# A rolling pipeline of attention tiles: the turned maxima move into the bank of the projections, and rounds of the loop end elsewhere

## What is computed

```python
xn = rmsnorm(x, norm_w)
q = (xn @ wq).reshape(T, 4, 4, 32)          # 16 query heads in 4 groups
k, v = cond @ wk, cond @ wv                 # 4 heads of 32 shared by the groups
attn = softmax(q @ k.T / sqrt(32))          # 512 x 512 for each of 16 heads
out = x + (attn @ v).reshape(T, 512) @ wo
```

## Time and profile before

| | us |
|---|---|
| median of 3 runs | 4432.54 (4431.65 to 4432.71) |
| profiled execution, its own time | 4432.37 |
| its span, first to last instruction | 4430.5 |
| TensorE busy | 4158.9 (94%) |
| VectorE busy | 2515.7 (57%) |
| ScalarE busy | 2077.2 (47%) |
| GpSimd busy | 2008.8 (45%) |
| DMA, share of 16 engines | 36% |

### The profile page before, as it was taken

One profiled execution on the slowest core, in us unless ns is written; L12 is line 12 of the kernel. 1 busy time (PEld: TensorE's weight loads), 2 busy tenths in 40 slices (PEclk: granted clock), 3 DMA queues, 4 the chain that ended last, 5 costly groups with the idle time before them and its releaser, 6 DMA issues.

```text
span 4430.5 us, 62098 instructions
## 1 busy us (share of the span) xinstructions
PE 4158.9 (94%) x19496; PEld 2654.1 (60%) x19496; DVE 2515.7 (57%) x3453; ACT 2077.2 (47%) x2648; POOL 2008.8 (45%) x1072
## 2 busy tenths in 40 slices
PE   9999999988999999999788999998999999899999
PEld 7888888874665566555444554554555555454555
DVE  3122200016556655566577777777777777777775
ACT  2111211114344444444265666665666666656665
POOL 0000000004555555565256665655666566656665
PEclk9999999998999999999899999999999999999999
DMA  5333522235444554454322322323222333223322
GB/s 182 132 128 136 160 87 82 93 96 138 119 127 124 130 132 118 126 136 130 96 81 69 81 78 81 90 81 88 75 81 77 89 90 91 73 75 81 85 74 66
DMA packets 316045, 451.72 MB, mean 102 GB/s; under 512 B 45176, under 2 KB 117368, under 8 KB 315832
## 3 DMA queue, kind: packets, MB, share of 16 engines
q1 hardware_dynamic: 315832, 448.86, 36.0%
HBM read 217.72 MB, written 102.77 MB: 72 GB/s over the span
## 4 chain that ended last, share of the span: by engine, by line
PE 37%; DVE 5%; ACT 5%; issue 4%; SPq 0%; POOL 0%; DVEq 0%; DMA 0%; ACTq 0%
PE a_ps L2017 9%; PE a_ps L2063 7%; PE a_ps L2049 6%; PE a_ps L2006 6%; PE a_ps L2086 5%; DVE a_max_cols L1885 3%; ACT a_q_ops L1769 2%; PE a_ps L2074 2%; PE a_ps L2079 2%; ACT a_probs L1778 2%; PE a_ps L2040 1%; PE a_ps L1992 1%; DVE a_stage L1904 1%; DVE x_lo L1895 1%; DVE wq_lo L1862 0%
## 5 line engine op out<-in xcount | busy, mean ns | idle before, releaser
L1885 DVE TENSOR_REDUCE a_max_cols<-a_ps 128x1 f32<-128x512 f32 x1536 | 1022.5, 672 | 421.2 <-PE a_ps L2017 415.4
L1778 ACT ACTIVATE a_probs<-a_ps 128x1024 f32<-128x1024 f32 x768 | 784.7, 1025 | 692.9 <-PE a_ps L2049 690.6
L2017 PE MATMUL a_ps<-a_k_ops,a_q_ops 96*128 96x512 f32 x1536 | 699.9, 457 | 110.1 <-DVE a_max_cols L1885 84.2
L1687 POOL TENSOR_TENSOR a_sums<-a_probs 128x1024 f32<-128x1024 f32 x192 | 454.5, 2386 | 412.2 <-ACT a_probs L1778 412.2
L2017 PEld LDWEIGHTS a_ps<-a_k_ops,a_q_ops 96*128 96x128 f32 x1536 | 296.9, 193 | 512.2 <-DVE a_max_cols L1885 273.5
L1036 DVE TENSOR_REDUCE a_max_cols<-a_ps 128x1 f32<-128x512 f32 x522 | 346.0, 686 | 351.0 <-PE a_ps L1189 351.0
L2049 PE MATMUL a_ps<-a_q_ops,a_k_ops 128*128 128x512 f32 x1536 | 494.7, 404 | 32.7 <-issue 32.0
L1687 POOL TENSOR_TENSOR a_sums<-a_sums,a_probs 128x1024 f32<-128x1024 f32 x192 | 463.9, 2436 | 19.8 <-ACT a_probs L1778 19.8
L803 POOL MEMSET a_ident<- 128x128 f32 x1 | 0.2, 204 | 976.5 <-issue 976.5
L2063 PE MATMUL a_ps<-a_probs,a_v 128*32 128x512 f32 x3072 | 428.6, 631 | 0.0
L303 DVE TENSOR_TENSOR cp_c_lo<-cp_raw,cp_c_hi 128x1024 fp32r<-128x1024 f32 x64 | 78.4, 1225 | 528.2 <-ACT cp_c_hi L247 528.1
(11 more groups left out here) (131 smaller groups left out, 7424.6 us busy)
## 6 DMA issues: line engine op xcount, KB each, us to landing
a_k_ops<-k_scratch SPq DMA_DIRECT2D x201, 256.0 KB, 4.0
a_q_ops<-a_qn_hi SPq DMA_DIRECT2D x768, 64.0 KB, 2.0
k_scratch<-cp_out SPq DMA_DIRECT2D x88, 512.0 KB, 2.8
a_q_ops<-a_qn_hi SPq DMA_DIRECT2D x268, 128.0 KB, 2.3
cp_raw<-in_ctx_t SPq DMA_DIRECT2D x64, 512.0 KB, 4.1
x_raw<-out_t SPq DMA_DIRECT2D x25, 1024.0 KB, 5.7
a_q_ops<-a_qn_lo SPq DMA_DIRECT2D x384, 64.0 KB, 2.0
a_x_res<-out_t SPq DMA_DIRECT2D x92, 256.0 KB, 2.9
```

The costliest lines, as they stand in the source:

```text
L1687: pool.tensor_tensor(sums[:, hp], (probs if n < H else sums)[:, hp], probs[:, n], ALU.add)\
L1778: act.activation(probs[:, n], ps[:, 2 * (n % 2):2 * (n % 2) + 2, :], ACT.Exp).then_inc(exped, 1)
L1885: dve.tensor_reduce(max_cols[:, t % 2, col:col + 1], bank(b), AX.X, ALU.max, negate=True)\
L2017: pe.matmul(bank(b), q_ops[0:SHIFT, s, h, q * P:(q + 1) * P], k_ops[0:SHIFT, s, :], start=True, stop=True).then_inc(smax, 1)
```

## The change

1. The turned maxima go into bank 7 (`FB`). `turn` waits for the 16 reductions of its tile and for the addition that empties the bank (`added`). The denominators of the tile before, which use the bank next, wait for both halves of `shift` in place of the addition.
2. The maxima alternate strictly over banks 4 and 5, and each waits for the reduction of the one two before it. The waits of M13, M14 and M15 change by that.
3. The order on TensorE becomes

GpSimd's and SyncE's streams stay as they are. The core of the diff:

```diff
-    OUTB, FB, TURNB = 6, 7, 5
+    OUTB, FB = 6, 7
...
-    MAXB = (4, 5, 4, 5, 4, 5, 4, 5, 4, 5, 4, 5, 4, 4, 4, 5)
...
         def turn_bank(it, t):
-            return FIRST_TURNB if isinstance(it, int) and it == 0 and t == 0 else TURNB
+            return FIRST_TURNB if isinstance(it, int) and it == 0 and t == 0 else FB
+
+        def max_bank(i):
+            return 4 + i % 2
...
+            def first_part(it, t, par):
+                exponential(it, t, 0)
+                if there(it, t - 2):
+                    round_output(*at(it, t - 2), par if t >= 2 else 1 - par)
+                if there(it, t - 1):
+                    take_outputs(*at(it, t - 1))
+                    take_denominators(*at(it, t - 1))
+                if t == 1:
+                    where(act, it, par, 1, lambda: round_wo(it // B))
+                exponential(it, t, 1)
...
+                maximum(it, t, 2)
+                if t == 1:
+                    where(dve, it, par, 1, lambda: rest_wo(it // B))
+                reciprocal(*at(it, t - 1), 0)
...
+                maximum(it, t, 10)
+                if t < T - 1 and there(it, t - LAG):
+                    add_result(it, t)
+
+            def second_part(it, t, par):
+                first = isinstance(it, int) and it == 0
+                if t == T - 1 and there(it, t - LAG):
+                    add_result(it, t)
+                maximum(it, t, 11)
+                reciprocal(*at(it, t - 1), 3)
...
+                maximum(it, t, 12)
+                if t == T - 1 and there(it, 2 * T):
+                    invert_mean_square(it + 2, 0)
+                if t == 0 and there(it, T):
+                    split_x(it + 1, 0)
+                maximum(it, t, 13)
+                if t == 0 and there(it, T):
+                    split_x(it + 1, 1)
+                maximum(it, t, 14)
...
             def batch(it, par):
...
+                    if there(it, t - 1):
+                        second_part(*at(it, t - 1), par if t > 0 else 1 - par)
+                    first_part(it, t, par)
...
                     no = tile_no(it, t) * M + LEAD + i
-                    if i == 15:
-                        pe.wait_ge(shifted, 2 * (tile_no(it, t) + 2))
-                    else:
-                        pe.wait_ge(reduced, no if i in (13, 14) else no - 1)
-                    one_maximum(*at(it, t_m), n, MAXB[i])
+                    pe.wait_ge(reduced, no - 1)
+                    one_maximum(*at(it, t_m), n, max_bank(i))
...
                 g = tile_no(it, t)
-                if isinstance(it, int) and g >= G - 1:
-                    pe.wait_ge(reduced, G * M)
+                pe.wait_ge(reduced, (g + 1) * M)
+                if there(it, t - LAG - 1):
+                    pe.wait_ge(added, g - LAG)
                 else:
-                    pe.wait_ge(reduced, (g - 1) * M + LEAD + 12)
+                    pe.wait_ge(q_taken, g + AHEAD)
+                    pe.wait_ge(ms_step, 2 * MS if t > 0 else 2 * MS + 1)
...
                 g = tile_no(it, t)
-                wait(pe, added, g - LAG + 1)
+                if there(it, t + 1):
+                    pe.wait_ge(shifted, 2 * (g + 2))
+                else:
+                    pe.wait_ge(added, g - LAG + 1)
                 for h in range(H):
```

More of the change, by code:

```diff
@@ L1810, in batch @@
[L1810 to L1820, removed]
@@ new lines, in second_part @@
+            def second_part(it, t, par):
+                first = isinstance(it, int) and it == 0
+                if t == T - 1 and there(it, t - LAG):
+                    add_result(it, t)
+                maximum(it, t, 11)
+                reciprocal(*at(it, t - 1), 3)
+                if t == 0 and first:
+                    for i in range(PARTS):
+                        invert_mean_square(1, i)
+                maximum(it, t, 12)
+                if t == T - 1 and there(it, 2 * T):
+                    invert_mean_square(it + 2, 0)
+                if t == 0 and there(it, T):
+                    split_x(it + 1, 0)
+                maximum(it, t, 13)
+                if t == 0 and there(it, T):
+                    split_x(it + 1, 1)
+                maximum(it, t, 14)
+                if t == T - 1 and there(it, 2 * T):
+                    invert_mean_square(it + 2, 1)
+                if t == 0 and there(it, T):
+                    split_x(it + 1, 2)
+                    where(dve, it, par, B - 1, lambda: rest_wq(it // B + 1))
+                maximum(it, t, 15)
@@ new lines, in first_part @@
+            def first_part(it, t, par):
+                scores(it, t, 0)
+                maximum(it, t, 0)
+                outputs(*at(it, t - 1), KT - 1, par if t > 0 else 1 - par)
+                denominators(*at(it, t - 1))
+                maximum(it, t, 1)
+                scores(it, t, 1)
+                maximum(it, t, 2)
+                project_q(*at(it, t + AHEAD), range(1))
+                maximum(it, t, 3)
+                project_q(*at(it, t + AHEAD), range(1, 2))
+                scores(it, t, 2)
+                maximum(it, t, 4)
+                project_q(*at(it, t + AHEAD), range(2, 3))
+                maximum(it, t, 5)
+                project_q(*at(it, t + AHEAD), range(3, 4))
+                scores(it, t, 3)
+                maximum(it, t, 6)
+                outputs(it, t, 0, par)
+                if isinstance(it, int) and it == 0 and t == 0:
+                    pe.wait_ge(q_taken, AHEAD + 1)
+                    sum_squares(1, FB)
+                if t == T - 1 and there(it, 2 * T):
+                    pe.wait_ge(q_taken, tile_no(it, t) + AHEAD + 1)
+                    sum_squares(it + 2, FB)
+                maximum(it, t, 7)
+                scores(it, t, 4)
+                maximum(it, t, 8)
+                if t < T - 1:
```

194 lines of the change are left out of this document (80 added, 114 removed).

## The result

The changed kernel takes 4276.97 us in the median of four runs (4267.27 to 4278.56) where the kernel before takes 4432.62 (4431.65 to 4435.84): ratio 0.9643, 95% interval 0.9626 to 0.966, 156 us less. The forecast was 4258 and the range 4225 to 4325, so it is faster as forecast, by 19 us less than that. The profiled execution has a span of 4274.2 us against 4430.5, again 156 less.

A forecast was written before the change was run, and what follows sets the result against it. The prediction took TensorE, and what keeps it waiting in the grouped layers' loop, as the bound. Its terms, 38+5+40+40+31+16+3 = 173, say 174, taken from 4432.4 gave 4258 us; range 4225 to 4325.

The forecast's parts named there:

- What bounds the kernel: Grouped layers' loop, 1857.1 us: TensorE is busy for 1731.7 us, so only what keeps it waiting counts.
- Alternation at t=1 and 2: Maxima 3, 14 and 15 in tiles t=1 and 2 wait less: net 0.79 us a tile, 38 us over 48 tiles.
- The denominators' wait: Denominators, reusing the turned maxima's bank, wait for the shifts: about 0.15 us a tile, bounds 0 and 1.1.
- the slower rival: Bank 7 becomes one chain and late shifts eat the gain: 4467 us at 2.2 us a tile; chance 0.04.
- t=3: Tiles t=3: same three gains, less new waits at maxima 9 and 14; net 0.2 us x 24, 5 us.
- t=0: Tiles t=0: splits of x one reduction later, shorter waits; 1.8 us less x 22, 40 us.
- Half clock: Time TensorE loses at half clock, mostly in the loop: 40 us gained, bounds 0 and 42.
- rival 1: Clock still falls behind the 0.9 us wait at t=0 and at round ends: 4302 us; chance 0.14.
- The output weights: Tiles rounding the output weights: earlier rounding and subtraction cost 4.8 us, not 10.3; 16 us over three times.
- The round's end: Loop's closing branch: twelve queued projection matmuls cover the fetch, about 0.95 us stays; 9 x 3.4 = 31 us gained.
- Rival 2: Fetch at the loop's closing branch is not covered, as the branch waits for the queue to drain: 4293 us; chance 0.10.
- Rivals 3 and 5: 3: splits blocked as before, t=0 gains nothing, 4328 us, chance 0.10; 5: waits only move, about 4432, chance 0.02.

## Why the prediction was right, and where it was off

*What bounds the kernel* held: TensorE's work did not change, and the gain is idle time and half clock.

*Alternation at t=1 and 2*: 0.79 us a tile predicted, 0.91 and 0.87 measured between undisturbed tiles (20.45 and 20.40 in the windows above; 20.5 had been forecast). Maximum 3 alone gave 0.34 of the 0.36. From maximum 10 to the next maximum 0 a tile t=2 takes 7.34 us where it took 8.02: 0.68 gained where 0.58 was predicted. The denominators' wait was sized rightly: 3.19 us from maximum 0 to 1 where 3.04 was usual, 0.15 more. Nothing waits on bank 7 in an ordinary tile otherwise, so the slower rival falls.

*t=3*: 0.2 predicted, -0.05 measured. The wait at maximum 9 is there as worked out, and so is one at 14:

```profile
3309.74 0.39 PE L2038 MATMUL a_ps<-a_k_ops,a_q_ops 96*128 96x512 f32 x1
3310.57 0.50 PE L2038 MATMUL a_ps<-a_k_ops,a_q_ops 96*128 96x512 f32 x1 [0.44 <-DVE a_max_cols L1895]
...
3318.19 0.49 PE L2038 MATMUL a_ps<-a_k_ops,a_q_ops 96*128 96x512 f32 x1 [0.36 <-DVE a_max_cols L1895]
```

Maximum 9 comes 0.83 us behind 8 where 0.23 is unhindered, the 0.6 of the prediction, and maximum 14 loses 0.28 where 0.25 stood. What was left out is the hole of 0.11 behind the wait at 9 and its like where the order of outputs 1 and maximum 11 is turned: 0.25 a tile, 6 us. That this is the price of the new order at t=3 is shown by the run in which the projection out is back between the maxima: t=3 is 0.92 us shorter there (0.16 of it comes back at t=0).

*t=0*: 1.8 predicted, 1.90 measured (23.06 to 21.17), with what the prediction left: maximum 0 of the next tile is 0.76 late, 0.9 with its hole had been forecast. t=0 and the next tile take 41.62 us; 42 had been forecast.

*Half clock*: 40 predicted. In the loop before, the t=0 tiles are 16 + 19 us above 23.06 and the t=1 tiles 4 above 21.36; after, all that is down to 2. So 37 of the loop's 39 us went, and rival 1 falls for these tiles. The granted clock of the loop is 0.99 and not 1.00 because of the tiles with a round's end and the output weights.

*The output weights*: 4.8 us a tile left over predicted; 2.8, 4.2 and 5.6 in the three tiles. The wait at maximum 5, predicted as 3.1, is 2.5 to 2.6 of idle time, with the subtraction taking 2.5:

```profile
2998.69 2.50 DVE L1872 TENSOR_TENSOR wq_lo<-a_w_raw,wq_hi 128x512 fp32r<-128x512 f32 x4 [0.91 <-ACT wq_hi L1743]
...
3002.65 0.79 PE L2038 MATMUL a_ps<-a_k_ops,a_q_ops 96*128 96x512 f32 x1 [2.53 <-DVE a_max_cols L1895]
```

This wait is the same in all three; what differs is the granted clock behind it, the third figure from the end of a window's line:

```profile
2303.99:2327.22 23.23, 20.55 (x109) 11.88 (x109) 19.16 (x29) 16.08 (x21) 13.20 (x7) 1.00 0.37 105
2992.70:3017.32 24.62, 22.01 (x108) 12.71 (x109) 18.88 (x29) 17.12 (x22) 13.26 (x7) 0.93 0.41 113
3685.80:3711.86 26.06, 23.46 (x109) 13.16 (x109) 18.88 (x29) 17.11 (x22) 13.32 (x7) 0.87 0.39 112
```

The second of these tiles in the kernel with its loop at instruction 64, with the same idle time of 2.52 us at maximum 5:

```profile
2988.64:3011.86 23.22, 20.62 (x109) 11.80 (x109) 18.68 (x29) 17.11 (x22) 13.24 (x7) 1.00 0.41 116
```

So half clock costs 0, 1.4 or 2.8 us here. The 1.7 of the prediction lies in the middle of that, by luck: nothing in it could tell which.

*The round's end* is the term that was mis-sized. The prediction let 0.95 of 4.35 us stay, 31 us gained. The 0.95 is there (0.94 above and 0.84 in the mean of nine, the branch 3.3 to 3.7 us, queued matmuls run on over it). But 3.36 us stay in all: in the mean 1.93 more before the turn, in the second fetch, and the remaining 0.6 at half clock. By the tile windows 6 us are gained, 25 fewer than predicted. The earlier trace rows counts the packets, nine in a round, and only the count was used; their times in the same trace would have shown two fetches close together at each round's start, and that a stall can follow the second if the end of the block comes early. The length of the code ahead of the loop was part of the change, and was priced at nothing. With the loop at instruction 64 the changed kernel takes 4254.67, near the forecast of 4258, which had described a round's end with one fetch; the other terms' misses nearly cancel.

The sum closes: 25 us too much for the ends of rounds and 5 for t=3 in the loop, less 6 too little for t=0, 1 and 2 there and 6 too little outside it, make 18 of the 19. (The prediction's own terms make 173; the 174 that it took is 1 more without a reason.) Rival 2 (4293) falls too: the fetch it spoke of is covered, another one is not. Rivals 3 and 5 fall by the rows of t=0.

The Trainium skill (Runtime: NRT & Kernel Launch, Instruction fetch mechanics) calls prefetch "purely sequential" and says that a taken branch whose target is outside the current two-page window forces a fetch of the target page. The trace of the grouped loop agrees, and adds the price: 3.3 to 3.7 us for most branches (4.7 at most), and up to 2.3 more where the page after the target is needed soon. The trace of layer 0 doesn't: its loop has 1316 instructions, five blocks by the estimate above, yet its branch takes 0.21 us, and between 1170 and 2140 us no packet of TensorE's instructions was loaded. The same section also names 128 KiB as TensorE's store. The grouped loop of 2043 instructions is 127.7 KiB by that count, and at instruction 0 it was still fetched in each round; the store may hold less of a loop than that, which was not tried.

## What to carry to other kernels

Where a loop is fetched anew in each round, the end of a round has two prices, the target's block and the one behind it. Put work that waits for nothing ahead of the branch, and look where the loop begins in its block before and after every edit, since here a change of the code ahead of the loop shifted it by some 20 us. A hint of the branch's target took both prices away. Price a VectorE step by which GpSimd instruction runs beside it, and place it where none does: the same piece took 0.68 or 2.35 us. And where a stall of some microseconds may or may not bring the clock down, a part of the measured gain is chance: compare tiles at the same granted clock.

## What the runs showed of the hardware

A branch whose target had been told ahead took 0.36 us and not 3.3 to 3.7, and no second stall followed. Without the hint, in the kernels before and after, the target's block was asked for 0.9 to 1.3 us after the branch began and TensorE went on 1.3 to 1.5 us after it had landed; the block behind it was asked for only 0.65 us or more later. The loops of the kernels before and after, 2031 and 2043 instructions, were fetched anew in each round wherever they began; the first layer's of 1316 is not.

A subtraction on VectorE that ran beside a GpSimd sum or product ended 0.55 us behind that one's end in the rows above, and took 1.65, 1.15 and 2.35 us, where it takes 0.68 alone.

Stalls of 1.3 us, one in each t=0 tile, left the clock at 2.4 GHz in 16 of 18 tiles, where two in a row had brought it down in 18 of 20. One stall of 2.5 us in the tiles with the output weights left it at 2.4 GHz or brought it to 1.2 for a part of the tile, in otherwise equal tiles. What decides between these cases was not tried further.
